# Attention's product moved into the scores' PSUM banks, the engines' orders rewritten, and the mask added by VectorE

## The reference, cut to what matters

```python
q, k, v = split(x @ Wqkv, 3)                   # 16 heads of 64
q, k = l2norm(q) * qs, l2norm(k) * ksc         # then rotated, with a scale by position
sim = einsum('wie,wje->wij', q, k2) * 8        # windows of 32 queries, 64 keys each
sim = where(mask, -max, sim)                   # causal, and no window ahead of the first
x = x + softmax(sim) @ v2 @ Wo                 # token shift on half of the columns
x = x + (a * gelu(gate)) @ W2                  # a, gate = split(layernorm(x) @ W1)
```

## Time and profile before

| | us |
|---|---|
| three runs, median (lowest to highest) | 2231.51 (2224.43 to 2232.05) |
| the profiled execution, its own time | 2231.53 |
| its span, first to last instruction | 2229.8 |
| busy: TensorE, VectorE | 1949.5, 1347.5 |
| busy: ScalarE, GpSimd | 1181.8, 1198.6 |

### The profile page before, as it was taken

The page is one execution under the profiler, slowest core; times in us unless marked ns, Lnnn a source line. Parts: engine busy times, 40 slices in busy tenths (PEclk is TensorE's granted clock), DMA queues, the critical chain, the costliest instruction groups (busy, mean ns, idle before and its releaser), DMA issues. The chain is left out here.

```text
span 2229.8 us, 70852 instructions
## 1 busy us (share of the span) xinstructions
PE 1949.5 (87%) x30532; PEld 1195.8 (54%) x30632; DVE 1347.5 (60%) x1564; ACT 1181.8 (53%) x2030; POOL 1198.6 (54%) x1291
## 2 busy tenths in 40 slices
PE   6868998899899889899988989999898899986898
PEld 5635555555455555555555555555555555553444
DVE  5647666666666666566665666666666666653443
ACT  4426555655555555465555556555555655653234
POOL 0229665675665576566666566756665665650000
PEclk8979999999999999999999999999999999998788
DMA  1023222322222222222222213222232222221000
GB/s 43 1 91 76 56 59 50 86 58 62 58 57 55 70 66 68 50 59 73 66 56 66 59 47 87 56 65 57 57 77 60 69 64 55 48 55 43 0 10 10
DMA packets 84767, 125.09 MB, mean 56 GB/s; under 512 B 26208, under 2 KB 31976, under 8 KB 84336
## 3 DMA queue, kind: packets, MB, share of 16 engines
q1 hardware_dynamic: 84464, 120.64, 21.5%
HBM read 21.98 MB, written 1.05 MB: 10 GB/s over the span
## 5 line engine op out<-in xcount | busy, mean ns | idle before, releaser
L320 POOL TENSOR_TENSOR qkn<-t 128x1024 f32<-128x1024 f32 x192 | 451.8, 2359 | 195.9 <-PE ring L392 118.5
L311 POOL TENSOR_TENSOR qkn<-qkn,rn 128x512 f32<-128x512 f32 x384 | 388.2, 1042 | 7.5
L392 PEld LDWEIGHTS ring<-ident,qkn 128*128 128x128 f32 x1536 | 181.7, 142 | 311.7 <-issue 265.1
L392 PE MATMUL ring<-ident,qkn 128*128 128x128 f32 x1536 | 237.9, 278 | 68.8 <-ACT gel L609 34.2
L440 PE MATMUL ring<-prT,v_win 64*64 64x32 f32 x12288 | 241.3, 222 | 64.5 <-issue 63.5
L440 PEld LDWEIGHTS ring<-prT,v_win 64*64 64x64 f32 x12288 | 213.7, 136 | 156.2 <-issue 144.6
L684 DVE TENSOR_REDUCE den<-pexp 128x16 f32<-128x1024 f32 x96 | 117.1, 1220 | 258.9 <-ACT pexp L546 258.9
L704 DVE TENSOR_TENSOR t<-qk_ps,rot 128x1024 f32<-128x1024 f32 x192 | 228.7, 1191 | 70.2 <-ACT sq L576 62.0
L328 POOL TENSOR_TENSOR pn<-pexp,rden 128x512 f32<-128x512 f32 x192 | 196.2, 1043 | 120.7 <-DVE rden L689 120.5
L670 DVE TENSOR_REDUCE smax<-sc_ps 128x16 f32<-128x1024 f32 x96 | 117.6, 1225 | 231.3 <-PE sc_ps L409 231.3
L370 PE MATMUL qk_ps<-wqkv,state 128*128 128x512 f32 x384 | 224.4, 669 | 14.4 <-DMA wqkv<-in_w_qkv 8.0
(11 more groups left out here) (238 smaller groups left out, 2910.5 us busy)
## 6 DMA issues: line engine op xcount, KB each, us to landing
v_win<-v_tok SPq DMA_DIRECT2D x1488, 64.0 KB
wqkv<-in_w_qkv SPq DMA_DIRECT2D x18, 512.0 KB, 3.8
wo<-in_w_o SPq DMA_DIRECT2D x6, 512.0 KB, 3.7
w<-in_w SPq DMA_DIRECT2D x6, 341.0 KB, 3.3
w<-in_w SPq DMA_DIRECT2D x6, 192.0 KB, 3.1
r_xtok<-in_x SPq DMA_DIRECT2D x4, 256.0 KB, 3.7
amask<-in_att_mask SPq DMA_DIRECT2D x1, 1024.0 KB
out_x<-xo SPq DMA_DIRECT2D x4, 256.0 KB, 2.3
```

The costliest lines, as they stand in the source:

```text
L311: nc.gpsimd.tensor_tensor(by_head(quarter(qkn, f)), by_head(quarter(qkn, f)), rn[:, 8 * f:8 * (f + 1)].unsqueeze(2).to_broadcast([P, 8, DH ...
L320: nc.gpsimd.tensor_tensor(half(qkn, k), half(t1, k), half(t2, k), ALU.add).then_inc((q_added, k_added)[k], 1)
L392: ins = nc.tensor.transpose(to[:, n * P:(n + 1) * P], qkn[:, c * P:(c + 1) * P], ident[:, :])
```

## The change

The two mask products and their bf16 operands go. The scores' products overwrite their banks, and VectorE adds the mask while it writes the scores to SBUF; it then takes the maximum from SBUF and subtracts it in place, again in two halves. Attention's result goes to the scores' banks between two tiles' scores and no longer to the ring; its two halves stand apart from each other in the first half of the stage. All five engines' orders, the ring's fills and GpSimd's order are new: V's first half is projected first of all in a stage and its second half near the end, K's two halves apart, Q and K's quarters are transposed as 1, 0, 2, 3, ScalarE squares Q straight after its projection, and VectorE rotates K last. `squares` of Q waits for the product and no longer for the rotation, which waits for the squares instead. SyncE waits in addition for an earlier tile's attention. In the diff, the lines that the orders had before are left out (they stand in the code above), and so are ScalarE's and VectorE's orders, which read afterwards:

- ScalarE: V 0, squares Q, exponentials 0, transposed quarters 1 and 0, exponentials 1, quarter 2, `centred`, gelu 0, attention 0, gelu 1, attention 1, quarter 3, squares K, gelu 2, `inverse_deviation`, `inverse_norms`, probabilities 0, V 1, probabilities 1.
- VectorE: `row_max`, `ffn_norm` (now in kind 0), rotate Q, `row_sum`, `add_ffn`, gated 0, sum Q, gated 1, sum K, gated 2, `add_attention`, rotate K.

```diff
@@ stage_fills: which product takes which ring bank, in TensorE's order
+            fills += [("v", g, 0)] * tile_there(g)
+            fills += [("t", g - 1, 1)] * tile_there(g - 1)
+            fills += [("t", g - 1, 0)] * tile_there(g - 1)
+            fills += [("t", g - 1, 2)] * tile_there(g - 1)
+            fills += [("w2", down, 0)] * (down is not None)
+            fills += [("xc", centre, 0)] * (centre is not None)
+            fills += [(k, up, 0) for k in ("gate", "lin")] * (up is not None)
+            fills += [(k, up, 1) for k in ("gate", "lin")] * (up is not None)
+            fills += [("t", g - 1, 3)] * tile_there(g - 1)
+            fills += [("wo", out_1, 1)] * (out_1 is not None)
+            fills += [("wo", out_0, 0)] * (out_0 is not None)
+            fills += [("var", spread, 0)] * (spread is not None)
+            fills += [(k, up, 2) for k in ("gate", "lin")] * (up is not None)
+            fills += [("p", g - 2, 0)] * tile_there(g - 2)
+            fills += [("v", g, 1)] * tile_there(g)
+            fills += [("p", g - 2, 1)] * tile_there(g - 2)
@@ SyncE, ahead of the moves of V
                     sp.wait_ge(v_copied, 2 * (g + 1))
+                    if g > 2:
+                        sp.wait_ge(av_full, g - 2)
@@ GpSimd's order
+                    if tile_there(g - 1):
+                        scale_qk(g - 1, 3)
                     if tile_there(g - 2):
+                        scale_p(g - 2, 0)
                     if tile_there(g):
+                        add_terms(g, 0)
+                    if tile_there(g - 2):
+                        scale_p(g - 2, 1)
+                    if tile_there(g):
+                        inverse_norms(g)
+                        scale_qk(g, 1)
+                        scale_qk(g, 0)
+                        add_terms(g, 1)
+                        scale_qk(g, 2)
@@ TensorE: project_v (project_k has the same with f == 1), scores, attend
+                    if f == 0:
+                        if g % (B * TILES) == 0:
+                            pe.wait_ge(s_wv, 16 * (g // (B * TILES) + 1))
+                        state_there(g)
...
-                        if g > 0:
-                            pe.wait_ge(sc_sub, 2 * g)
-                        for par in range(2):
-
-                            nc.tensor.matmul(sc_ps[:, par, :], ident_bf[:, :], mask_bf[:, int(t > 0), :, :],
-                                             start=True, stop=False, skip_group_check=True)
+                        if g == 1:
+                            pe.wait_ge(sc_taken, 2)
+                        if g > 1:
+                            pe.wait_ge(oT_copied, 2 * (g - 1))
...
-                                    start=False, stop=True, skip_group_check=True)
+                                    start=True, stop=True)
...
+                        pe.wait_ge(sc_taken, 2 * min(g + 2, TILE_COUNT))
...
-                                        to[part][64 * par:64 * (par + 1), P * pair + WIN * q:P * pair + WIN * (q + 1)],
+                                        sc_ps[64 * par:64 * (par + 1), part, P * pair + WIN * q:P * pair + WIN * (q + 1)],
@@ TensorE's order
+                    if tile_there(g):
+                        project_v(g, 0)
+                        project_q(g, 0)
+                        project_q(g, 1)
+                    if tile_there(g - 3):
+                        attend(g - 3, 0)
+                    if tile_there(g - 1):
+                        transpose_qk(g - 1, 1)
+                        transpose_qk(g - 1, 0)
+                    if tile_there(g):
+                        project_k(g, 1)
+                    if tile_there(g - 1):
+                        transpose_qk(g - 1, 2)
+                    if down is not None:
+                        ffn_down(down)
                     if centre is not None:
                         ffn_centre(centre)
                     if up is not None:
                         ffn_up(up, 0)
+                    if tile_there(g - 3):
+                        attend(g - 3, 1)
                     if up is not None:
                         ffn_up(up, 1)
+                    if tile_there(g - 1):
                         transpose_qk(g - 1, 3)
+                    if tile_there(g):
+                        project_k(g, 0)
+                    if out_1 is not None:
+                        output_projection(out_1, 1)
                     if out_0 is not None:
                         output_projection(out_0, 0)
+                    if spread is not None:
+                        ffn_variance(spread)
                     if up is not None:
                         ffn_up(up, 2)
+                    if tile_there(g - 1):
+                        scores(g - 1, 0)
+                    if tile_there(g - 2):
+                        transpose_p(g - 2, 0)
+                    if tile_there(g):
+                        project_v(g, 1)
+                    if tile_there(g - 1):
+                        scores(g - 1, 1)
+                    if tile_there(g - 2):
+                        transpose_p(g - 2, 1)
@@ ScalarE: squares
-                    if k == 0:
-                        act.wait_ge(q_rot, 2 * (g + 1))
-                    else:
-                        act.wait_ge(k_full, 2 * (g + 1))
+                    act.wait_ge((q_full, k_full)[k], 2 * (g + 1))
@@ VectorE: row_max
-                    nc.vector.tensor_reduce(smax[:, :], sc_ps[:, :, :].rearrange("p a n -> p (a n)").rearrange("p (h k) -> p h k", k=64), AX.X, ALU.max).then_inc(max_ready, 1)
-                    dve.wait_ge(max_ready, g + 1)
...
+                    by_rows = pr[:, :].rearrange("p (n r k) -> p n r k", r=2, k=64)
...
                             sc_ps[:, :, :].rearrange("p a (h k) -> p a h k", k=64)[:, :, pairs, :],
-                            smax[:, :].rearrange("p (a h) -> p a h", a=2)[:, :, pairs].unsqueeze(3).to_broadcast([P, 2, 4, 64]), ALU.subtract).then_inc(sc_sub, 1)
+                            mask_f[:, int(g % TILES > 0):int(g % TILES > 0) + 1, :].unsqueeze(2).to_broadcast([P, 2, 4, 64]), ALU.add).then_inc(sc_taken, 1)
+                    dve.wait_ge(sc_taken, 2 * (g + 1))
+                    nc.vector.tensor_reduce(smax[:, :], by_head(pr[:, :]), AX.X, ALU.max).then_inc(max_ready, 1)
+                    dve.wait_ge(max_ready, g + 1)
+                    for f in range(2):
+                        nc.vector.tensor_tensor(by_rows[:, :, f, :], by_rows[:, :, f, :],
+                                                smax[:, :].rearrange("p (n r) -> p n r", r=2)[:, :, f:f + 1].to_broadcast([P, 8, 64]), ALU.subtract).then_inc(sc_sub, 1)
```

More of the change, by code:

```diff
@@ L151, in build_network @@
         TILE_COUNT = ROUNDS * TILES
-        STAGES = TILE_COUNT + 6
+        STAGES = TILE_COUNT + 7
+        turn_at = {f: n for n, f in enumerate((1, 0, 2, 3))}
+        scale_at = {f: n for n, f in enumerate((1, 0, 2, 3))}
         def tile_there(g):
@@ L428, in attend @@
                     t = g % TILES
-                    to = [bank_of("a", g, part) for part in range(2)]
                     if f == 0:
@@ L432, in attend @@
                         pe.wait_ge(v_moved[t], moves_of[t] * (g // TILES + 1))
-                        for part in range(2):
-                            ring_bank("a", g, part)
+                        pe.wait_ge(sc_taken, 2 * min(g + 2, TILE_COUNT))
                     for pair in range(2 * f, 2 * (f + 1)):
@@ L483, in _ @@
                 for g in range(STAGES):
-                    now, turn, prob, att = (tile_there(g - n) for n in range(4))
-                    up, down = round_at(g, 0, 2), round_at(g, 1, 2)
-                    out_0, out_1, centre = round_at(g, 1, 1), round_at(g, 2, 1), round_at(g, 3, 1)
-                    for f in range(2):
-                        if att:
-                            attend(g - 3, f)
-                        if now:
-                            project_q(g, f)
+                    out_0 = round_at(g, 1, 1)
@@ L518, in _ @@
-                    if now:
-                        project_v(g, 1)
-                    if out_1 is not None:
-                        output_projection(out_1, 1)
+                    if spread is not None:
+                        ffn_variance(spread)
                     if up is not None:
                         ffn_up(up, 2)
-                    for f in range(2):
-                        if prob:
-                            transpose_p(g - 2, f)
-                        if turn:
-                            scores(g - 1, f)
+                    if tile_there(g - 1):
+                        scores(g - 1, 0)
@@ L644, in _ @@
                         nc.scalar.preload_act_table_set(LN_EXP_SET)
-                    for f in range(2):
-                        if prob:
-                            copy_pT(g - 2, f)
-                    if now:
+                    if spread is not None:
+                        inverse_deviation(spread)
+                    if tile_there(g):
```

(6 more changed lines are left out.)

195 lines of the change are left out of this document (77 added, 118 removed).

## The result

The changed kernel takes 2110.49 us (median; 2109.57 to 2111.79), the kernel before 2228.64 beside it: a ratio of 0.9471, 95% interval 0.945 to 0.9492. That is 118 us less, where 98 had been forecast (2134; the range was 2070 to 2240).

What follows compares the result with a forecast made beforehand. TensorE's order bounds the kernel. A stage of 17.0 + 0.5 + 0.28 = 17.8 us against 19.6 saves 173 in 96 stages; layer starts cost 75: 2231.5 - 173 + 75 = 2134 us, range 2070 to 2240 (the forecast's own 2090 to 2195).

Steps and rivals of the forecast that it cites:

- forecast floor of 17.0: TensorE's busy time per stage after the change: 17.66 - 0.5 - 0.36 + 0.2 = 17.0 us.
- tails: Extra time TensorE's small products last around a pause, beyond its idle time: 0.5 us of the busy 17.66 a stage.
- The orders: New engine orders together with the mask's move: a stage of 17.8 us against 19.6, 173 us saved in 96 stages.
- the layer starts: TensorE waits 13.8 us for V weights, plus 2.3 for a slow clock, less 1.2: 14.9 x 5 = 75 us.
- the remaining issue pauses: TensorE's pauses without a visible semaphore, at small products: a quarter stays, 0.28 us a stage, between 0 and 1.05.
- the new waits: TensorE's waits for the ring and the banks, in kinds 0, 2 and 3: 2.1 us a round, 0.5 a stage.
- Rival A: TensorE's issue pauses stay and cost 1.05 us a stage instead of 0.28: 2208 us, between 2195 and 2240; 15%.
- VectorE's new work: Two new subtractions in SBUF at 0.82 us each: VectorE from 12.44 to 14.1 us a stage, still below TensorE.
- Rival B: VectorE becomes the bound, its subtractions standing behind GpSimd instructions: 17.5 us, with waits 19.5 a stage, 2297 us; 14%.
- Rival C: All TensorE pauses go and layer starts cost 13 x 5 = 65 us: 2046 us, to 2090; 11%.
- The ring and SyncE: TensorE's 31.4 us of ring waits behind gelu go; SyncE's moves of V, 11.9 us, stay hidden with 3 left.
- the norm's loop: Chain from K's second product through the norm's scaling to the next K: 13.7 us, under the stage, nothing charged.

Runs made afterwards that it cites:

- Experiment 3: Changed kernel with the mask back on TensorE as two mask products, all orders and banks as changed: 2056.47 us, ratio 0.9197.
- experiment 8: Changed kernel with the mask back on TensorE and two buffers for the V weights: 1997.07 us, ratio 0.8926.
- (7): Kernel before the change, with both Q products moved ahead of both attention halves: 2224.86 us, ratio 0.9943.
- (6): Changed kernel with attention's second half directly behind its first: 2128.04 us, ratio 0.9512.
- experiment 2: Changed kernel with two buffers for the V weights, so the next layer's load comes ahead of the last tile's work: 2058.2 us, ratio 0.9225.
- 9: Changed kernel with no row maximum and two buffers for the V weights: 1987.12 us, ratio 0.8892.
- experiment 4: Changed kernel without the row maximum and its subtractions in the softmax: 2036.27 us, ratio 0.9114.
- experiment 5: Changed kernel with VectorE's layer norm step ahead of the maximum in stages of kind 0: 2086.13 us, ratio 0.9332.

## Why the prediction was right, and where it was not

**TensorE sets the time: right, with a limit.** With the mask on TensorE a round is 67.5 us, 16.9 a stage, all but 0.37 us of it busy. The forecast floor of 17.0, which was without the mask's 0.36, was 0.5 too high. One of its terms was misread: "with two to three pauses a stage" gave tails of 0.5, but the earlier trace rows has 92 issue pauses in 84 stages, which makes 0.2. Since the floor came out lower all the same, the busy time held more to gain than that reading saw; no run prices the tails and the 0.2 for changes between large and small products apart.

**The orders: right in kind, too small in size.** Experiment 3 holds what the orders and the banks did with the mask left where it was: 178 us less than the 2234.8 of before beside it. The 59 us that the layer starts cost (8 against 3) are in it, so the orders alone brought some 237; experiment 8, without either cost, is 240 us below the kernel before beside it. The sum had 173 for orders and mask together, 138 without the mask's 0.36 x 96. Three terms were too careful: the floor (0.5 a stage), the remaining issue pauses (0.28 a stage, 27 us) and the new waits, 0.5 a stage, of which experiment 3 shows 0.37 in a whole round.

**The issue pauses: right cause, remainder mis-sized.** I had a quarter stay (0.28 a stage, 27 us). None stayed: the 18.1 us that the whole changed trace labels "issue" stand in front of L475 and are the wait for the norm, but for one of 2.8 that every version shows. That the place of the small products makes them is shown from both sides, in direction: spread in the kernel before they fall by 50 us (7), and with attention's halves together some come back (6). Only 8.3 of 78.6 us do, so the size hangs on more than those two halves. That it is the supply of instructions that lags there stays an argument; no run here shows it. Rival A is out: about as many instructions, and no pause. Its sentence on the Trainium skill (Runtime: NRT & Kernel Launch, section on instruction fetch mechanics), by which the fetching of instructions is hidden by the issue rate, is neither borne out nor refuted by that, since the cause itself was not tested.

**The layer starts: right mechanism, price too high.** The sum had 14.9 us each, 75 in all; measured by taking most of the wait away, 52 (experiment 2), 49 (9 against 4) and 59 (8 against 3). The wait is 12.4 us (61.9 in 5) instead of 13.8. The slow clock after it is there (2.08 for the first V product; 0.77 over the next 6.3 us). But the pause lets VectorE and GpSimd get ahead, and the stage behind it takes 18.6 to 19.5 us instead of 20.8 to 22.3: 2.5 back in the mean, where I had put 1.2. The changed trace's own stages agree: 13.4 longer than others of kind 3, less 2.5, is 54 us in five.

**VectorE's new work: the step that failed.** "Their nearest row is the one product with two SBUF operands, 0.82 ... I take 0.82". It was 1.58, and VectorE came to 15.73 us a stage instead of 14.1. I also said that "the row shows a lengthening and no such blocks". The row could not show them, as the timeline of before says once one looks at what GpSimd did at that moment:

```profile
970.79 2.37 POOL L320 TENSOR_TENSOR qkn<-t 128x1024 f32<-128x1024 f32 x1 [0.74 <-DVE t L708]
...
972.88 0.83 DVE L731 TENSOR_TENSOR xc<-xc,xsq 128x512 f32<-128x512 f32 x1
```

The norm's product began 0.28 us before GpSimd's instruction ended (at 973.16) and itself ended at 973.71, 0.55 us after. In experiment 3 it began 2.12 before the end (970.55) and ended at 971.10, again 0.55 after; in the changed kernel GpSimd ended at 927.85 and VectorE at 928.39, 0.54 after. So it was blocked each time, and only the moment differed: 0.83 was a late arrival, not a small effect. The Trainium skill, SBUF — State Buffer, section "Who interferes with whom", says that whichever of the two starts first has the shared port pair for its whole instruction and the other fully blocks. The trace agrees: 2.67 us for an instruction that takes 0.68 in experiments 4 and 5. Also the block is inside the duration shown, not in the idle time ahead of it, where I had looked for it.

**Rival B: its mechanism came true, its sign did not.** VectorE's load rose to 15.7 and not to the 17.5 that it supposed, since a subtraction stood 0.9 us behind GpSimd in the mean and not 1.7. It did not become the bound of every stage, but of kind 0: maximum, subtractions and norm in a row hold up the feed-forward (experiment 5: 24 us), and the mask's part as a whole turned from a gain of 35 into a loss of 54 us (experiment 3).

**Rival C: two of its conditions came true.** No issue pause stayed, and the layer starts cost less than 65 us. What held the time above its 2090 is the mask's loss.

**The ring and SyncE: right; the norm's loop: too tight.** Kind 2 has no wait left, and of kind 3's 0.88 us 0.7 is already the wait for the V weights. TensorE never waits for the moves. For the norm's loop "0.6 us or more under the stage everywhere, so nothing is charged" did not hold: TensorE waits for the scaled Q and K 19.9 us in the 84 stages, one of the prediction's own signs of being wrong. The margin was less than what the blocks add to GpSimd's instructions. With the mask on TensorE these waits are 14.0 in the whole program instead of 35.4; without the maximum (experiment 4) they are 26.9, for there the norm's product still lengthens GpSimd's in kind 0.

So the total was near the forecast by luck: errors cancelled. The orders gave some 100 us more (237 to 240 for 138). The mask and the layer starts together cost 113 us (2110 against experiment 8), where the sum had 75 - 35 = 40: the starts 52 to 59 of them instead of 75, the mask 54 to 61 where 35 had been its gain, by which of the two is taken away first.

## What to carry to other kernels

When an instruction's price is read from a row, look at what the engine that shares a resource with it did in those very microseconds: a mean of 24 instances at one phase is one sample, not 24. Before moving work off the bounding engine, ask what its new form does to a third engine; here 0.43 us a stage saved on TensorE made VectorE and GpSimd block each other and cost more than it saved. A load that stands behind a queue's routine moves is priced by where its consumer stands in the order, so it has to be checked again whenever that consumer moves. And stages are compared with the spread of their kind, not with one of them.

## What the runs showed of the hardware that I had not expected

- VectorE's instruction with two SBUF operands waits for the whole of a running GpSimd instruction: 2.67 us instead of 0.68, ending 0.55 us after it in three kernels. The reverse is there too: GpSimd's sum of terms took 2.81 instead of 2.36, and its small first step 0.61 in the kernel before behind the norm's product, where it takes 0.28.
- The norm's second instruction, with a single SBUF tensor operand, is held up as well: 1.12 us in experiment 3 against 0.55 at its shortest, so a single tensor operand is no safeguard.
- Issue pauses of TensorE depend on how closely small products stand: 78.6 us in the kernel before, 28.4 with two Q products moved in between, 8.3 in front of attention with its halves together in the changed kernel, none there with them apart. What in that causes them is not shown.
- Pauses of 1.4 and 1.1 us close together can lower TensorE's clock: in 8 of 16 stages of kind 0 it stood at 0.92 in the mean (0.50 from 931 to 933 us), in the other 8 at 1.00, and the first are 1.2 to 1.5 us longer.
